# A layer tower of window attention, experts and retention: scores ahead of projection in one loop, retention output ahead of gates in another

## The chip, the cores and the metric

The kernel runs on one core of a Trainium2 chip. The metric is the device time of one execution in microseconds; several executions are timed and their median is compared.

## What is computed

The input is x, 4 x 64 x 64 x 64, that is 16384 tokens of 64 channels. Five parts follow one another; all but the first add to their input.

```python
h = _L0_tok_ref(x, ...)                       # 8x8 windows, rotary attention, 8 heads of 8
h = h + _L0_attn_ref(_layernorm(h), ...)      # 7x7 local attention on the 64x64 grid, 8 heads
h = h + _L0_ffn_ref(_layernorm(h), ...)       # relu(h Wi), two layers of shared + routed expert, Wo
h = h + _L1_attn_ref(_layernorm(h), ...)      # retention: (q k^T / 8 * decay mask) v, causal
h = h + _L1_ffn_ref(_layernorm(h), ...)       # gate > 0.5 over 8 experts, sign(x) @ sign(sum of weights)
```

## The kernel before

All activations stay in one tile `h` (128 partitions, 128 tiles of tokens, 64 channels). Each engine has its own program, written out by hand, and the order of the work on an engine is the order of its code. Engines meet at semaphores that count: `pe.wait_ge(T2["exp_done"], ...)` and the like. An engine that waits holds everything behind it in its program. There are three stages.

The first does the window attention for 32 pieces of 512 tokens. The change does not touch it.

**The merged loop** does the local attention for 64 strips of 4 image rows (256 tokens; index i, in pairs `(j, par)`), and makes, five strips ahead (`LEAD`), the keys, queries and values of strip m = i + 5 from the first stage's rows (the "pre" work). On TensorE (`strip` under `tensor`) a strip is: `scores(0)` (L784, L788), the first half of the attention scores, transposed, into PSUM banks S0 and S1; `peak(.., 0)` (L761, L765), scores of the next strip for its row maxima; `pre_turn` (L733), two transposes of normalized rows; `project` of strip i - 1 (L827); `pre_values` (L741); `scores(1)`, the second half, into the same two banks; `peak(.., 1)`; `values(0)` (L807, L813), sums and weighted values of the first half; `pre_keys` (L749); `turn_maxima` (L773); `values(1)`. ScalarE (`weights`, L1137) takes the exponentials, two instructions for each half, and copies `xnp` (L1093), `v_sb` (L1099), `kpad` (L1104) and `mT` (L1108) out of PSUM; it also issues the loads of `v_patch` (`values_in`, L1126) in its queue. VectorE takes the maxima (L1327), adds the projection to `h` (`residual`, L1341), makes the pre work's statistics (`pre_moments`), and divides the values by their sums (`weigh`, L1332 and L1335, which writes `aT`). GpSimd builds `key_patch` and `q_block` two strips ahead; SP's queue moves keys and queries through memory.

Some waits matter for the change. `project` waits for `attn_out`, that is `aT` of the strip before. `scores(1)` waits until both exponentials of `scores(0)` have read the banks. `values(0)` waits for `v_sb` of the pre values of the same strip, as both use the PSUM bank OT:

```python
if g == 0:
    pe.wait_ge(T2["v_in%d" % par], times((j + 1) * 48))
    pe.wait_ge(T2["attn_out"], times(i))
    pe.wait_ge(L["v_sb"], times(made(j, par)))
```

**The last stage** runs the feed-forward, the retention and the binary experts over 64 strips of 256 tokens as one staggered pipeline: in step j, strip f = j - 1 is in the feed-forward, r = j - 2 in the retention, b = j - 3 gets its retention output added, g = j - 4 its gates, and q = j - 6 its binary weights, 8 units of matmuls (`weights(k)`, L877) into two double banks in turn, each followed by a sign on ScalarE (`sign(k)`, L1165) or, for unit 1, a clip on VectorE (L1416). `reduce` (L894) sums two units. Within a step TensorE does unit 1, transposes (L917), units 2 and 3, the first feed-forward and the gates' matmul (L935, L937), `reduce`, the transposes of the retention's rows (L947) into bank OT, L953, unit 4, the retention's products (L963, L965), unit 5, L985, the spread of x over the gates (L995), L1003, L1005, `w_o` (L1011), unit 6 and `reduce`, unit 7, the retention output (L1027, L1028) into OT, and unit 0 of the next strip. L947 waits until VectorE has added the retention output of step j - 1 to `h` (L1429) from that same bank. VectorE takes the clip, normalizes the retention's rows (L1236), scales them (`kd`, L1421, L1422), compares the gates (L1426, waits for L937), and adds the retention output. SP's queue loads the expert's weights (L451), stores the result (L456) and copies the gated signs `xg` in 12 pieces to where units 0 to 7 read them (L463); the next `xg` (L1452) waits for those copies.

Of the kernel before, what the change touches and what calls it, by code (L numbers as in the profile page):

```python
# [11 lines left out]
ALU = mybir.AluOpType  # L12
# [110 lines left out]
def build(nc, a, out):  # L123
    ctx = ExitStack()
    with ctx:
# [459 lines left out]
        def _(pe):  # L585
# [254 lines left out]
            def strip(j, par):  # L840
                i = j * 2 + par
                m = ahead(j, par)
# [4 lines left out]
                if m is not None:  # L847
                    pre_turn(m)
                if not first:
                    project(i - 1, min(i + LEAD, NS) if isinstance(i, int) else i + LEAD)  # L850
                if m is not None:
                    pre_values(m, 1 - par)
                scores(j, par, 1)
                if not last:
# [13 lines left out]
            def strips(j, par):  # L868
# [128 lines left out]
                if r is not None:  # L997
# [6 lines left out]
                    for t in range(2):  # L1004
                        mm = pe.matmul(bank["OT"][:, 384 + t * C:384 + (t + 1) * C], kd3[:, t, :], v3[:, t, :], start=True, stop=True)  # L1005
                    mm.then_inc(RT["s_ps"], 1)
                if f is not None:
                    pe.wait_ge(FF["hid_sb"], times(f * 3 + 3))
                    settle(pe)
                    for t in range(2):  # L1010
                        mm = pe.matmul(bank["J1"][:, t * C:(t + 1) * C], hidT[:, 2, t * P:(t + 1) * P], w_o[:, :], start=True, stop=True)  # L1011
                    mm.then_inc(FF["out_ps"], 1)

                if q is not None:
                    signed(q, 5)
                    weights(6, par, unit(6, par))
                    reduce(q, 2)
                if g is not None:
# [24 lines left out]
        def _(act):  # L1043
# [84 lines left out]
            def strip(j, par):  # L1128
# [15 lines left out]
                if more:  # L1144
                    values_in(i + 1, 1 - par, 0)
                if m is not None:
                    pre_values(m, j + 2 + par, 1 - par)
                if more:
                    values_in(i + 1, 1 - par, 1)
                weights(1)  # L1150
                if m is not None:
                    pre_keys(m, j + 2 + par, 1 - par)
                if more:
# [5 lines left out]
            def strips(j, par):  # L1159
# [37 lines left out]
                if r is not None:  # L1197
                    act.wait_ge(RT["ud"], times(r + 1))
                    act.activation(v3[:, :, :], bank["OT"][:, 256:384].rearrange("p (t c) -> p t c", t=2), ACT.Copy).then_inc(RT["v"], 1)
                if f is not None:  # L1200
                    act.wait_ge(FF["hid_ps"], times(f * 3 + 3))
                    act.activation(hidT[:, 2, :], bank["J1"][:, 0:256], ACT.Relu, bias=w_exp[:, 1, HID:HID + 1]).then_inc(FF["hid_sb"], 1)

                if q is not None:
                    for k in range(5, 8):
                        sign(k)
# [5 lines left out]
        def _(dve):  # L1212
# [142 lines left out]
            def strip(j, par):  # L1355
# [5 lines left out]
                if not last:  # L1361
                    maxima(i + 1, 0)
                if not first:
                    residual(i - 1)
                if more:
                    pre_moments(nxt)
                if not last:
# [42 lines left out]
            def strips(j, par):  # L1410
# [6 lines left out]
                if r is not None:  # L1417
# [3 lines left out]
                    dve.tensor_scalar(kd3[:, 0, 0:C + 1], xn_r[:, 0, 0:C + 1], decay_k[:, :], None, ALU.mult).then_inc(RT["kd"], 1)  # L1421
                    dve.tensor_scalar(kd3[:, 1, 0:C + 1], xn_r[:, 1, 0:C + 1], decay_k[:, :], keep[:, 0, bass.ds(r, 1)], ALU.mult, ALU.mult).then_inc(RT["kd"], 1)  # L1422
                if g is not None:
                    dve.wait_ge(BN["g_ps"], times(g + 1))
                    dve.wait_ge(BN["xg"], times(g))
                    dve.tensor_scalar(gates[:, :], bank["T"][:, 0:256], b_gate[:, 0:1], 0.0, ALU.add, ALU.is_gt).then_inc(BN["gates"], 1)  # L1426
                if b is not None:
                    dve.wait_ge(RT["out_ps"], times(b + 1))
                    dve.tensor_tensor(rows(b * 2, 2), bank["OT"][:, 256:384].rearrange("p (t c) -> p t c", t=2), rows(b * 2, 2), ALU.add).then_inc(RT["h_done"], 1)  # L1429
                    dve.wait_ge(RT["h_done"], times(b + 1))  # L1430
# [114 lines left out]
```

## Time and profile before

| | |
|---|---|
| median of 3 runs | 1858.53 us (1854.55 to 1858.99) |
| the profiled execution | 1851.32 us, of which the span of instructions is 1849.4 us |
| mean granted clock of TensorE | 0.966 |
| TensorE matmul / weight load busy | 1651.0 us (89%) / 1224.2 us (66%) |
| VectorE, ScalarE, GpSimd busy | 1242.8 us (67%), 978.1 us (53%), 489.4 us (26%) |
| DMA | 139.23 MB, mean 75 GB/s |

Busy time is a share of the whole span and says little about a stage. The first stage ends at about 388 us, the merged loop's strips run from 425 to about 1003 us, the last stage from there to the end, with all its parts at work from about 1060 to 1780 us. The rows below show a wait as "idle before, and who ended it"; "issue" is time for which the profile names nobody. Ends of matmuls are modelled, and each block of matmuls starts some 0.07 to 0.2 us before the modelled end of the one ahead.

### The profile page before, as it was taken

To read this page: it belongs to the slowest core of one execution; us is meant where nothing else is said; L and a number is where in the kernel's file an instruction comes from. 1 tells how busy PE (TensorE), PEld (TensorE's weight loads), DVE (VectorE), ACT (ScalarE), POOL (GpSimd) and SP (SyncE) were. 2 spreads that over 40 slices of the span, in tenths; PEclk is the share of its full clock that TensorE was granted. 3 is DMA by queue.
4 is the path that set the end of the run, shared out by engine and by line. 5 is a ranking of instruction groups with operands and counts; after the bars stand their busy time and mean duration, and the time that the engine had idled before them with its cause. 6 is when DMAs were issued, how large, how long until landed. Compare 5 with 4: busy or idle time off the path is not lost.

```text
span 1849.4 us, 93991 instructions
## 1 busy us (share of the span) xinstructions
PE 1651.0 (89%) x35754; PEld 1224.2 (66%) x35754; DVE 1242.8 (67%) x3477; ACT 978.1 (53%) x1861; POOL 489.4 (26%) x605
## 2 busy tenths in 40 slices
PE   5899999968999999999996799999999999999986
PEld 3566666656777777777775566666666666666663
DVE  2556566655777777777764677777777777777772
ACT  2344444422333333333332277777777777777776
POOL 2200000015555555555542221222122212221210
PEclk8899999968999999999998799999999999999998
DMA  3100000004334444443342133333333333333332
GB/s 97 53 11 14 11 11 11 16 22 112 109 109 112 112 115 113 114 111 110 109 111 61 33 80 80 78 78 83 80 78 77 85 79 78 77 85 78 78 77 60
DMA packets 146983, 139.23 MB, mean 75 GB/s; under 512 B 58754, under 2 KB 106498, under 8 KB 146658
## 3 DMA queue, kind: packets, MB, share of 16 engines
q1 hardware_dynamic: 138594, 112.03, 23.9%
q10 hardware_dynamic: 8320, 26.22, 5.0%
q8 instruction: 50, 0.82, 0.2%
q14 instruction: 19, 0.16, 0.0%
HBM read 62.38 MB, written 16.99 MB: 43 GB/s over the span
## 4 chain that ended last, share of the span: by engine, by line
PE 81%; issue 8%; DVE 5%; SPq 2%; ACT 2%; DMA 1%; POOL 1%; DVEq 0%; ACTq 0%; POOLq 0%
PE ps_D L877 11%; PE ps_D L788 7%; PE ps_OT L807 4%; PE ps_D L666 4%; PE ps_J L827 4%; DVE prob L1416 4%; PE ps_AV L813 3%; PE ps_AV L894 3%; PE ps_D L784 3%; PE ps_J L953 2%; PE ps_J L749 2%; PE ps_OT L741 2%; PE ps_J L985 2%; PE ps_J L620 2%; PE ps_J L935 2%
## 5 line engine op out<-in xcount | busy, mean ns | idle before, releaser
L1165 ACT ACTIVATE prob<-ps_D 128x1024 bf16<-128x1024 f32 x448 | 450.6, 1022 | 80.9 <-PE ps_D L877 80.5
L1137 ACT ACTIVATE prob<-ps_D 100x512 f32<-100x512 f32 x256 | 138.7, 594 | 219.5 <-PE ps_D L788 219.5
L515 POOL TENSOR_TENSOR rstd_pre<-veps_pre,minus_half 128x2 f32<-128x2 f32 x64 | 44.8, 700 | 560.3 <-DVE veps_pre L1224 560.3
L1327 DVE TENSOR_REDUCE m_sb<-ps_D 128x4 f32<-128x400 f32 x256 | 134.6, 567 | 76.4 <-PE ps_D L765 76.3
L788 PE MATMUL ps_D<-tile_a,key_patch 64*100 64x128 f32 x2048 | 174.6, 288 | 1.2 <-issue 1.2
L1290 DVE TENSOR_REDUCE top<-ps_D 128x8 f32<-128x512 f32 x128 | 79.4, 682 | 143.1 <-PE ps_D L639 143.1
L877 PE MATMUL ps_D<-tile_b,w_parts 128*128 128x256 bf16 x1024 | 154.5, 274 | 15.7 <-DVE prob L1416 7.7
L877 PE MATMUL ps_D<-tile_a,w_parts 128*128 128x256 bf16 x1024 | 153.9, 273 | 14.0 <-DVE prob L1416 7.5
L788 PEld LDWEIGHTS ps_D<-tile_a,key_patch 64*100 64x100 f32 x2048 | 136.3, 166 | 1.6 <-issue 1.5
L531 POOL TENSOR_TENSOR tile_a<-q_st,q_mask 128x1024 f32<-128x1024 f32 x64 | 123.5, 1930 | 30.0 <-DMA q_st<-q_d 15.6
L1416 DVE TENSOR_SCALAR prob<-ps_D 128x1024 bf16<-128x1024 f32 x64 | 78.3, 1224 | 76.5 <-PE ps_D L877 76.5
L784 PE MATMUL ps_D<-mT,key_rows 64*100 64x128 bf16 x1024 | 121.3, 227 | 9.2 <-issue 8.7
L515 POOL TENSOR_TENSOR rstd_bin<-veps_bin,minus_half 128x2 f32<-128x2 f32 x64 | 44.1, 689 | 313.4 <-DVE veps_bin L1224 313.4
L877 PEld LDWEIGHTS ps_D<-tile_b,w_parts 128*128 128x128 bf16 x1024 | 87.3, 99 | 55.0 <-issue 42.3
L877 PEld LDWEIGHTS ps_D<-tile_a,w_parts 128*128 128x128 bf16 x1024 | 87.1, 99 | 53.6 <-issue 40.5
L515 POOL TENSOR_TENSOR rstd_ret<-veps_ret,minus_half 128x2 f32<-128x2 f32 x64 | 46.5, 727 | 237.7 <-DVE veps_ret L1224 237.7
L661 PE MATMUL ps_D<-top_T,top_rows 32*64 32x64 bf16 x2048 | 90.3, 193 | 19.6 <-ACT top_T L1071 14.7
L1075 ACT ACTIVATE prob<-ps_D 128x512 f32<-128x512 f32 x128 | 69.5, 595 | 72.1 <-PE ps_D L666 72.0
L894 PE MATMUL ps_AV<-prob,lane_sum 128*32 128x256 bf16 x2048 | 103.4, 279 | 1.2 <-ACT prob L1165 1.2
L1452 DVE TENSOR_TENSOR xg<-ps_D,gates 128x1024 bf16<-128x1024 f32 x64 | 78.3, 1224 | 37.0 <-PE ps_D L995 25.7
L827 PE MATMUL ps_J<-w_p,aT 64*32 64x64 f32 x4096 | 70.4, 217 | 36.5 <-issue 36.5
L827 PEld LDWEIGHTS ps_J<-w_p,aT 64*32 64x32 f32 x4096 | 61.8, 107 | 51.0 <-issue 50.8
(175 smaller groups left out, 3989.7 us busy)
## 6 DMA issues: line engine op xcount, KB each, us to landing
tile_a<-xg SPq DMA_DIRECT2D x384, 64.0 KB, 2.0
tile_b<-xg SPq DMA_DIRECT2D x384, 64.0 KB, 2.0
key_st<-k_d SPq DMA_DIRECT2D x128, 162.0 KB
tile_b<-v_d ACTq DMA_DIRECT2D x128, 120.0 KB
tile_b<-v_d ACTq DMA_DIRECT2D x64, 160.0 KB
w_exp<-experts SPq DMA_DIRECT2D x64, 129.0 KB, 2.3
xin<-in_x SPq DMA_DIRECT2D x32, 128.0 KB, 2.2
k_d<-kpad SPq DMA_DIRECT2D x64, 64.0 KB, 2.8
```

Of the source, the lines that this page charges most:

```text
L515: gp.tensor_tensor(rstd[:, :], veps[:, :], minus_half[:, 0:veps.shape[1]], ALU.pow).then_inc(q["rstd"], 1)
L531: gp.tensor_tensor(q_block[:, par, :].rearrange("c (p h q) -> c p h q", h=NH, q=NQ), q_st[:, :].rearrange("c (p a q) -> c p a q", a=1, q=N ...
L661: pe.matmul(s_tok[j][m, at], top_half(top_rows[r, p * 2 + e, :]), top1_T[r, m], start=True, stop=False)
L784: pe.matmul(s_loc[x][0:NKL, u * P:(u + 1) * P], top_half(key_rows[rows_of(x), par, at * NKL:(at + 1) * NKL]), mT[rows_of(x), par, :], star ...
L788: mm = pe.matmul(s_loc[x][0:NKL, u * P:(u + 1) * P], key_patch[rows_of(x), par, at * NKL:(at + 1) * NKL], q_block[rows_of(x), par, at * P: ...
L827: mm = pe.matmul(bank["J1"][at:at + 32, t * C:(t + 1) * C], aT1[rows_of(x), a4 * P + 32 * r:a4 * P + 32 * (r + 1)], w_p2[rows_of(x), a4, : ...
L877: mm = pe.matmul(d[:, a * 512 + oh * 256:a * 512 + (oh + 1) * 256], w_parts[:, at, oh, :, :].rearrange("r i o -> r (i o)"), x_parts[half][ ...
L894: mm = pe.matmul(bank["AV"][32 * cg:32 * (cg + 1), 0:256], lane_sum[:, int(k == 1), :], sgn[:, k % 4, cg * 256:(cg + 1) * 256], start=k == ...
L1137: act.activation(prob1[0:NKL, 2 * g + x, :], s_loc[x][0:NKL, :], ACT.Exp).then_inc(T2["exp_done"], 1)
L1165: act.activation(sgn[:, k % 4, :], unit(k, par)[:, :], ACT.Sign).then_inc(BN["sign"], 1)
L1327: dve.tensor_reduce(m_sb[:, C * x + HOT[x] + 4 * g:C * x + HOT[x] + 4 * g + 4], m_loc[x][:, 0:4 * NKL].rearrange("p (u n) -> p u n", u=4), ...
L1416: dve.tensor_scalar(sgn[:, 1, :], unit(1, par)[:, :], -TINY, TINY, ALU.max, ALU.min).then_inc(BN["clip"], 1)
```

## The change

In the merged loop, TensorE's `scores(1)` moves from behind `pre_values` to behind `pre_turn`. ScalarE's copy of the pre values moves from between two DMA issues to behind the second exponentials. VectorE's `pre_moments` moves ahead of `residual`.

In the last stage, TensorE's unit 6 and its reduction move ahead of `w_o`, ScalarE's `sign(5)` ahead of the last hidden Relu, and VectorE's add of the retention output ahead of the gates. No instruction is added or taken away.

```diff
@@ merged loop, TensorE
                 if m is not None:
                     pre_turn(m)
+                scores(j, par, 1)
                 if not first:
                     project(i - 1, min(i + LEAD, NS) if isinstance(i, int) else i + LEAD)
                 if m is not None:
                     pre_values(m, 1 - par)
-                scores(j, par, 1)
                 if not last:
                     peak(*after(j, par), 1)
                 values(j, par, 0)
@@ last stage, TensorE
+                if q is not None:
+                    signed(q, 5)
+                    weights(6, par, unit(6, par))
+                    reduce(q, 2)
+
                 if f is not None:
                     pe.wait_ge(FF["hid_sb"], times(f * 3 + 3))
                     settle(pe)
                     for t in range(2):
                         mm = pe.matmul(bank["J1"][:, t * C:(t + 1) * C], hidT[:, 2, t * P:(t + 1) * P], w_o[:, :], start=True, stop=True)
                     mm.then_inc(FF["out_ps"], 1)
-
-                if q is not None:
-                    signed(q, 5)
-                    weights(6, par, unit(6, par))
-                    reduce(q, 2)
@@ merged loop, ScalarE
                 if more:
                     values_in(i + 1, 1 - par, 0)
-                if m is not None:
-                    pre_values(m, j + 2 + par, 1 - par)
-                if more:
                     values_in(i + 1, 1 - par, 1)
                 weights(1)
                 if m is not None:
+                    pre_values(m, j + 2 + par, 1 - par)
                     pre_keys(m, j + 2 + par, 1 - par)
@@ last stage, ScalarE
+                if q is not None:
+                    sign(5)
                 if f is not None:
                     act.wait_ge(FF["hid_ps"], times(f * 3 + 3))
                     act.activation(hidT[:, 2, :], bank["J1"][:, 0:256], ACT.Relu, bias=w_exp[:, 1, HID:HID + 1]).then_inc(FF["hid_sb"], 1)
 
                 if q is not None:
-                    for k in range(5, 8):
+                    for k in range(6, 8):
                         sign(k)
@@ merged loop, VectorE
+                if more:
+                    pre_moments(nxt)
                 if not first:
                     residual(i - 1)
-                if more:
-                    pre_moments(nxt)
@@ last stage, VectorE
+                if b is not None:
+                    dve.wait_ge(RT["out_ps"], times(b + 1))
+                    dve.tensor_tensor(rows(b * 2, 2), bank["OT"][:, 256:384].rearrange("p (t c) -> p t c", t=2), rows(b * 2, 2), ALU.add).then_inc(RT["h_done"], 1)
                 if g is not None:
                     dve.wait_ge(BN["g_ps"], times(g + 1))
                     dve.wait_ge(BN["xg"], times(g))
                     dve.tensor_scalar(gates[:, :], bank["T"][:, 0:256], b_gate[:, 0:1], 0.0, ALU.add, ALU.is_gt).then_inc(BN["gates"], 1)
                 if b is not None:
-                    dve.wait_ge(RT["out_ps"], times(b + 1))
-                    dve.tensor_tensor(rows(b * 2, 2), bank["OT"][:, 256:384].rearrange("p (t c) -> p t c", t=2), rows(b * 2, 2), ALU.add).then_inc(RT["h_done"], 1)
                     dve.wait_ge(RT["h_done"], times(b + 1))
```

How the instructions stand on TensorE in the body of the merged loop before the change, from the pre turn to the first matmuls of `scores(1)` (names of semaphores: `loc_` local attention, `pre_` the pre work; `prob` holds exponentials):

```order
L733 MATMUL ps_T<-ident,xn 64x128 [waits pre_xn,pre_xT_sb]
L733 MATMUL ps_T<-ident,xn 64x128
L827 MATMUL ps_J<-w_p,aT 32x64 [waits loc_h_done,loc_attn_out,pre_k_sb,pre_q_sb]
L827 MATMUL ps_J<-w_p,aT 32x64 x31
L737 REGISTER_ALU
L741 MATMUL ps_OT<-w_v,xnp 128x64 [waits pre_xT_sb,pre_v_sb]
L741 MATMUL ps_OT<-w_v,xnp 128x64
L784 MATMUL ps_D<-mT,key_rows 100x128 [waits loc_exp_done]
L784 MATMUL ps_D<-mT,key_rows 100x128
L788 MATMUL ps_D<-tile_a,key_patch 100x128 x2
```

And in the changed kernel, the same place, from the last matmuls of `scores(1)` to `values(0)`:

```order
L784 MATMUL ps_D<-mT,key_rows 100x128 x2
L788 MATMUL ps_D<-tile_a,key_patch 100x128 x2
L827 MATMUL ps_J<-w_p,aT 32x64 [waits loc_h_done,loc_attn_out,pre_k_sb,pre_q_sb]
L827 MATMUL ps_J<-w_p,aT 32x64 x31
L737 REGISTER_ALU
L741 MATMUL ps_OT<-w_v,xnp 128x64 [waits pre_xT_sb,pre_v_sb]
L741 MATMUL ps_OT<-w_v,xnp 128x64
L757 REGISTER_ALU
L761 MATMUL ps_D<-key_rows,q_rows 128x400 [waits loc_max_done]
L761 MATMUL ps_D<-key_rows,q_rows 128x400
L765 MATMUL ps_D<-key_patch,tile_a 128x100 x8
L807 MATMUL ps_OT<-prob,ones_h 32x4x4x4 [waits loc_exp_done,pre_v_sb,loc_v_in1,loc_attn_out]
```

The scores, whose first matmul waits for `loc_exp_done`, now stand directly behind the pre turn, and between the pre values and `values(0)`, which waits for `pre_v_sb`, only L761 and L765 are left.

VectorE in the last stage before the change, from the clip to the statistics:

```order
L1416 TENSOR_SCALAR prob<-ps_D 128x1024 [waits bin_y_part,bin_w_ps]
L1236 TENSOR_SCALAR xn_r<-h,mv_ret,rstd_ret 128x64 [waits ret_xT_ps,ret_rstd]
L1236 TENSOR_SCALAR xn_r<-h,mv_ret,rstd_ret 128x64
L1421 TENSOR_SCALAR kd<-xn_r,decay_k 128x65 [waits ret_xn,ret_s_ps]
L1422 TENSOR_SCALAR kd<-xn_r,decay_k,keep 128x65
L1426 TENSOR_SCALAR gates<-ps_T,b_gate 128x256 [waits bin_xg,bin_g_ps]
L1429 TENSOR_TENSOR h<-ps_OT,h 128x128 [waits ret_out_ps]
L1218 BN_STATS stats_bin<-h 128x6 [waits ret_h_done]
```

In the changed kernel (where L1425 is the add and L1429 the gates):

```order
L1421 TENSOR_SCALAR kd<-xn_r,decay_k 128x65 [waits ret_xn,ret_s_ps]
L1422 TENSOR_SCALAR kd<-xn_r,decay_k,keep 128x65
L1425 TENSOR_TENSOR h<-ps_OT,h 128x128 [waits ret_out_ps]
L1429 TENSOR_SCALAR gates<-ps_T,b_gate 128x256 [waits bin_xg,bin_g_ps]
L1218 BN_STATS stats_bin<-h 128x6 [waits ret_h_done]
```

The add, which waits for the output of the step before, has changed places with the gates, which wait for this step's matmul.

## Rows read from the trace of the kernel before

**Rows 1.** The page, busy us (share of the span) xinstructions.

```profile
PE 1651.0 (89%) x35754; PEld 1224.2 (66%) x35754; DVE 1242.8 (67%) x3477; ACT 978.1 (53%) x1861; POOL 489.4 (26%) x605
```

**Rows 2.** Stretches: length, busy us (x instructions) by engine, clock, DMA share, GB/s.

```profile
415.00:1000.00 585.00, 529.73 (x16966) 450.47 (x16966) 405.02 (x911) 203.06 (x497) 293.65 (x309) 0.98 0.39 110
1060.00:1780.00 720.00, 667.89 (x6281) 467.54 (x6280) 541.95 (x1981) 547.38 (x869) 148.72 (x234) 1.00 0.33 80
```

**Rows 3.** TensorE's waits, 425 to 1000 us: total us, times, longest.

```profile
PE ps_J L827 <- issue: 34.6, 60, 0.8
```

**Rows 4.** Time line of two strips of the merged loop: start us, us, engine, line.

```profile
707.71 0.26 PE L784 MATMUL ps_D<-mT,key_rows 64*100 64x128 bf16 x2
...
709.19 1.08 ACT L1137 ACTIVATE prob<-ps_D 100x512 f32<-100x512 f32 x2 [1.98 <-PE ps_D L788]
...
709.43 0.41 PE L733 MATMUL ps_T<-ident,xn 128*64 128x128 f32 x2
...
709.71 0.69 DVE L1335 TENSOR_TENSOR aT<-ps_AV,rec 128x512 f32<-128x512 f32 x1
...
710.62 1.10 PE L827 MATMUL ps_J<-w_p,aT 64*32 64x64 f32 x64 [0.78 <-issue]
...
711.64 0.69 PE L741 MATMUL ps_OT<-w_v,xnp 128*128 128x64 f32 x4
...
712.26 0.26 PE L784 MATMUL ps_D<-mT,key_rows 64*100 64x128 bf16 x2
...
712.46 0.28 ACT L1099 ACTIVATE v_sb<-ps_OT 128x128 f32<-128x128 f32 x1 [1.93 <-PE ps_OT L741]
...
713.53 0.34 PE L761 MATMUL ps_D<-key_rows,q_rows 64*128 64x400 bf16 x2
...
713.98 0.65 PE L807 MATMUL ps_OT<-prob,ones_h 100*32 100x64 f32 x32
...
717.12 0.26 PE L784 MATMUL ps_D<-mT,key_rows 64*100 64x128 bf16 x2 [0.27 <-issue]
...
718.68 1.08 ACT L1137 ACTIVATE prob<-ps_D 100x512 f32<-100x512 f32 x2 [2.40 <-PE ps_D L788]
...
722.95 0.65 PE L807 MATMUL ps_OT<-prob,ones_h 100*32 100x64 f32 x32
...
725.75 0.26 PE L784 MATMUL ps_D<-mT,key_rows 64*100 64x128 bf16 x2
```

**Rows 5.** Time line of the last strip: TensorE waits for the exponentials.

```profile
1001.54 1.08 ACT L1137 ACTIVATE prob<-ps_D 100x512 f32<-100x512 f32 x2 [1.96 <-PE ps_D L788]
1002.77 0.44 PE L807 MATMUL ps_OT<-prob,ones_h 100*32 100x64 f32 x17 [0.25 <-ACT prob L1137]
```

**Rows 6.** TensorE's waits, 1060 to 1780 us.

```profile
PE ps_OT L947 <- issue: 32.9, 58, 0.6
```

**Rows 7.** Time line of one step of the last stage.

```profile
1401.12 0.48 DVE L1426 TENSOR_SCALAR gates<-ps_T,b_gate 128x256 f32<-128x256 f32 x1 [0.42 <-PE ps_T L937]
1401.53 0.28 DVE L1429 TENSOR_TENSOR h<-ps_OT,h 128x128 f32 x1
...
1401.91 0.41 PE L947 MATMUL ps_OT<-ident,xn_r 128*128 128x128 f32 x2 [0.53 <-issue]
...
1406.26 1.22 DVE L1452 TENSOR_TENSOR xg<-ps_D,gates 128x1024 bf16<-128x1024 f32 x1 [0.49 <-PE ps_D L995]
...
1407.97 1.94 ACT L1165 ACTIVATE prob<-ps_D 128x1024 bf16<-128x1024 f32 x2 [0.86 <-PE ps_D L877]
...
1409.40 1.25 PE L877 MATMUL ps_D<-tile_a,w_parts 128*128 128x256 bf16 x8
...
1412.16 0.60 PE L877 MATMUL ps_D<-tile_a,w_parts 128*128 128x256 bf16 x4 [0.27 <-DVE prob L1416]
```

**Rows 8.** SP's queue in the same step, in the same time line.

```profile
1408.76 6.26 SPq L463 DMA_DIRECT2D tile_b<-xg  x10
```

**Rows 9.** DMA issues of the page: engine, count, KB each, us to landing.

```profile
tile_b<-xg SPq DMA_DIRECT2D x384, 64.0 KB, 2.0
```

## The prediction, made before the changed kernel was run

> **What bounds the kernel now.** I read the page first: TensorE is busy 1651.0 us of the span, or 89% [rows 1]; no other engine passes 67%. The table of stretches then splits the span: the merged loop, 415 to 1000 us, has TensorE busy 529.73 of 585 us, and the full strips of the last stage, 1060 to 1780 us, 667.89 of 720 us, with a granted clock of 0.98 and 1.00 [rows 2]. So in both stages that the change touches, a microsecond in which TensorE does not stand still is a microsecond of the kernel, and work of the other engines counts only where TensorE waits for it. The list of waits names two such places. In the merged loop TensorE stood idle before `project` (L827) 60 times, 34.6 us in all, 0.58 us each [rows 3]. In the last stage it stood idle before the transposes of L947 58 times, 32.9 us, 0.57 us each [rows 6]. The change aims at both.
>
> The time lines show what ends these waits. In a strip that starts at 707.71 us, TensorE runs first scores, first maxima scores, and the pre turn at 709.43, and is through at about 709.8. `project` needs `aT`, which VectorE writes from 709.71 for 0.69 us, to 710.40; it starts at 710.62 [rows 4]. In the last stage VectorE has waited 0.42 us for the gates' matmul, since 1400.70; gates run 1401.12 to 1401.60, the retention add 1401.53 to 1401.81, and only then, at 1401.91, the transposes start, because they write the PSUM bank that the add reads [rows 7]. The add's own input was made in the strip before. It stands in the queue behind the gates for nothing.
>
> **Part 1, the merged loop.** `scores(1)` is put into the gap, ahead of `project` and `pre_values`. Nothing is added: blocks of TensorE change places, so only waits can change. Lengths, start to start [rows 4]: project 711.64 - 710.62 = 1.02; pre values 712.26 - 711.64 = 0.62; scores 713.53 - 712.26 = 1.27; maxima scores 713.98 - 713.53 = 0.45. Together 3.36 from project to `values(0)`.
>
> The new order has two waits. First, `scores(1)` writes the two banks that the exponentials of `scores(0)` read. They run 709.19 to 710.27, and from the end of an exponential to TensorE it is 0.15 us (1002.62 to 1002.77 [rows 5]), so `scores(1)` starts at 710.42, where `project` started at 710.62: 0.20 us earlier. In the next strip, which starts after the loop's branch, they end at 719.76, so it starts at 719.91; `project` started 3.36 before 722.95, at 719.59: 0.32 us later. Project itself then waits for nothing: it comes 1.27 us after that, and `aT` was there at 710.40.
>
> Second, `values(0)` waits for the copy `v_sb` of the pre values, since they share a PSUM bank. Today that copy ends 712.74, 1.10 us after the pre values started, hidden by scores(1). Behind the pre values there now stand only the maxima scores: 0.62 + 0.45 = 1.07 us, against 1.10 + 0.15 = 1.25. That is a new wait of 0.18 us in each strip. ScalarE's new order (the copy behind the second exponentials) costs nothing: exponentials end 2.56 us after their scores start (707.71 to 710.27 [rows 4]), and the pre values are done 1.27 + 1.02 + 0.69 = 2.98 us after `scores(1)` starts.
>
> So one strip of a pair changes by -0.20 + 0.18 = -0.02 and the other by +0.32 + 0.18 = +0.50; a pair, today 9.41 + 8.63 = 18.04 us, grows by 0.5. Over 29 pairs that is +14 us. In the last five strips there is no pre work. There `project` now lies beside the exponentials and hides their wait; moved behind, its 1.02 us come on top: +5, less 1 for the first strip, where the pre values today wait for their copy. The merged loop: **+18 us**. The queues: on ScalarE the second DMA issue of `v_patch` moves ahead of the copy, some 1.5 us earlier, at a time when the queue waits anyway. VectorE's `pre_moments` before `residual` costs nothing: after the first maxima VectorE would stand until `project`, which ends 1.3 us later than now, and the moments (about 1 us) fill that. It hides `residual` from `maxima(1)` as before, and GpSimd gets its input sooner.
>
> A rule of the Trainium skill (Perfetto Trace Analysis, Matmuls) speaks against this part: independent groups of matmuls should rotate through PSUM banks, so that the evacuation of one lies under the next group. Here two groups that use the same two banks come together. By that rule taken alone all of the 1.08 us of exponentials would be bare, and this is the last rival below.
>
> **Part 2, the last stage.** The add ahead of the gates: it runs from 1400.70 for 0.28 us, to about 1401.0, and nothing in it waits. The gates still start at 1401.12, when their matmul is done. So the transposes follow the block before them (0.53 us recorded as gap, 0.60 counted start to start, since blocks overlap by 0.07 [rows 7]): TensorE comes **0.59 us** earlier. What is late next? I walked one strip with the durations of today. (a) Unit 6 of the gate weights and its reduction move ahead of `w_o`, and on ScalarE `sign(5)` ahead of the last hidden Relu. Today sign 6 and 7 run 1407.97 to 1409.91, and the second half of the eight weight matmuls from 1409.40 (unit 1 of the next strip) needs sign 7: ScalarE is level with TensorE there [rows 7]. With the move unit 6 is about 0.46 us, one block of `w_o`, sooner, sign 6 starts about 1.05 us earlier and sign 7, behind unit 7, some 0.6; unit 1 then starts on time or 0.02 late. Without the move sign 7 would stand behind sign 6 and come 0.05 later: the move is worth little. (b) Unit 7 waits for `xg`, 1406.26 to 1407.48; that shifts by 0.6 with TensorE, and unit 7 too. (c) Unit 3 waits for the clip on VectorE, 0.27 us as now [rows 7]: it hangs on unit 1 and shifts with it. (d) The next `xg` waits for twelve copies of this one by SP's queue. They start at 1408.76, ten issues take 6.26 us, and one lands 2.0 us after its issue [rows 8, 9]: the last at 1408.76 + 11 x 0.626 + 2.0 = 1417.6. The next `xg` starts at 1406.26 + 12.4 = 1418.7 (58 steps in 720 us are 12.4 each [rows 2, 6]). In the new order that is 1.2 us sooner (twice 0.6), and the copies only 0.4, as SP first takes the expert's weights behind the last hidden Relu. Of 1.0 us in hand 0.2 is left. (e) `w_o` comes 0.86 us later against its neighbours; `h` of the feed-forward is added after the state update anyway, and its statistics have over a microsecond before the next use.
>
> Thus 58 strips by 0.59 = 34 us, and 1 for the strips at both ends: **-35 us**.
>
> **Sum.** +18 - 35 = -17 us. The profiled execution took 1851.3 us; it would take 1834. The median of the runs is 1858.5, 7 us above the profiled one; against it the forecast is **1841.5 us**, 0.9% faster. A difference of 0.3% (5.6 us) is what a measurement of this kernel can tell.
>
> **Rivals.**
> 1. *The last stage gives only half.* Speaks for it: three things are level within 0.1 us after the walk (sign 7, the state update before L1027, the copies by SP's queue). If any is 0.3 us later than I think, the gain is 0.3 a strip, 17 us. Then +18 - 17: about 1859 us. Against: each was taken with measured durations. Chance 0.15.
> 2. *The merged loop costs nothing.* If the wake of TensorE overlaps its weight load, or the exponentials start sooner, both new waits shrink by 0.15 and the gain of the even strip cancels the loss. Then -35: about 1824 us. Chance 0.16.
> 3. *The exponentials lie bare* (the slower one). Place: before `scores(1)` in the merged loop. The first maxima scores (0.45) and the pre turn (0.41, less 0.07 of overlap) are 0.79 us of work under the exponentials. If they are held themselves (by the maxima or by GpSimd's patches), the cover is gone and each of 63 strips pays 0.79 more, 50 us: 1858.5 - 17 + 50 = 1891 us. It decides from 0.36 us of lost cover a strip, where 23 us more bring the sum to +0.3%. Against: in rows 4 the turn follows without a gap, and nothing that feeds it moves later. Chance 0.07.
>
> **Numbers.** Forecast 0.62, rivals 0.15, 0.16, 0.07. The forecast's own spread is 1830 to 1853 (merged loop +8 to +25, last stage -36 to -30). The range 1824 to 1860 takes in rivals 1 and 2 and leaves out rival 3 and the far tails. Faster by over 0.3%: nearly all of the forecast, rival 2 and a little of rival 1, 0.79; within 0.3%: most of rival 1 and the edge of the forecast, 0.12; slower: rival 3 and the rest of 1, 0.09.
>
> **What would show it.** The idle time before L947 gone from the waits, gates behind the add, and a full step of the last stage 0.6 us shorter than today's 12.4. In the merged loop: no idle before `project`, but about 0.6 us before the second scores and 0.1 to 0.2 before `values(0)`, and a pair of strips of 18.5 us instead of 18.04. The forecast is wrong if a pair takes 18.1 or less (rival 2), if those steps stay above 12.05 us (rival 1), or if the gap before the second scores passes 1.1 us (rival 3).

## The result

The kernel before takes 1858.16 us (median; 1854.55 to 1858.99), the changed one 1843.87 us (1842.19 to 1845.71). The ratio is 0.9927, 95% interval 0.991 to 0.9944: 0.7% faster, where 0.9% was forecast. The profiled execution of the changed kernel took 1842.19 us, its span is 1840.2 us, 9.1 less than before.

The page, busy us by engine, answers to [rows 1]:

```profile
PE 1665.6 (91%) x35754; PEld 1227.2 (67%) x35754; DVE 1202.4 (65%) x3477; ACT 976.0 (53%) x1861; POOL 488.3 (27%) x605
```

The table of stretches, with the columns of [rows 2]:

```profile
415.00:1000.00 585.00, 524.53 (x16217) 436.10 (x16219) 359.45 (x910) 198.85 (x492) 288.26 (x309) 0.98 0.41 108
...
1060.00:1780.00 720.00, 696.14 (x6467) 490.01 (x6467) 569.54 (x2093) 560.58 (x902) 158.74 (x246) 0.99 0.34 82
```

TensorE's busy time in 720 us of the last stage rose from 667.89 to 696.14; in 585 us of the merged loop it fell from 529.73 to 524.53 (the changed kernel enters this loop 6.5 us later in its profile, see below). One stage gained and the other lost.

TensorE's waits from 425 to 1030 us, the merged loop (total us, times, longest), against [rows 3]:

```profile
PE ps_D L784 <- ACT prob L1137: 41.0, 64, 1.3
PE ps_D L784 <- issue: 8.7, 28, 1.5
```

The 34.6 us before `project` (L827) are gone. In their place stand 41.0 us before the second scores (L784), which wait for the exponentials. The `issue` row of L784 is the loop's branch, 0.27 us in every other strip, as in [rows 4].

Two strips on the time line, as in [rows 4]:

```profile
714.25 0.26 PE L784 MATMUL ps_D<-mT,key_rows 64*100 64x128 bf16 x2 [0.26 <-issue]
...
715.81 1.08 ACT L1137 ACTIVATE prob<-ps_D 100x512 f32<-100x512 f32 x2 [2.39 <-PE ps_D L788]
...
717.04 0.26 PE L784 MATMUL ps_D<-mT,key_rows 64*100 64x128 bf16 x2 [0.66 <-ACT prob L1137]
...
718.40 1.10 PE L827 MATMUL ps_J<-w_p,aT 64*32 64x64 f32 x64
...
719.43 0.68 PE L741 MATMUL ps_OT<-w_v,xnp 128*128 128x64 f32 x4
...
720.04 0.35 PE L761 MATMUL ps_D<-key_rows,q_rows 64*128 64x400 bf16 x2
720.15 0.28 ACT L1099 ACTIVATE v_sb<-ps_OT 128x128 f32<-128x128 f32 x1 [0.48 <-PE ps_OT L741]
...
720.64 0.65 PE L807 MATMUL ps_OT<-prob,ones_h 100*32 100x64 f32 x32
...
721.67 0.70 PE L749 MATMUL ps_J<-xnp,w_kq 128*128 128x256 f32 x2
...
722.20 0.27 PE L773 MATMUL ps_T<-ident,m_sb 128*128 128x128 f32 x1
722.41 0.65 PE L807 MATMUL ps_OT<-prob,ones_h 100*32 100x64 f32 x32
...
723.44 0.26 PE L784 MATMUL ps_D<-mT,key_rows 64*100 64x128 bf16 x2
...
726.15 0.26 PE L784 MATMUL ps_D<-mT,key_rows 64*100 64x128 bf16 x2 [0.58 <-ACT prob L1137]
```

The exponentials end at 716.89, the second scores start at 717.04: the forecast 0.15 us. `values(0)` starts 0.21 us after the `v_sb` copy ends (720.43 to 720.64); 1.21 us after the pre values.

TensorE's waits from 1070 to 1750 us, the last stage, against [rows 6]:

```profile
PE ps_D L877 <- DVE prob L1416: 4.0, 26, 0.2
...
PE ps_OT L947 <- DVE h L1425: 0.6, 1, 0.6
```

The wait before L947 is gone but for one. A step of the last stage, against [rows 7, 8]:

```profile
1400.76 0.48 DVE L1429 TENSOR_SCALAR gates<-ps_T,b_gate 128x256 f32<-128x256 f32 x1 [0.29 <-PE ps_T L937]
...
1400.95 0.44 PE L947 MATMUL ps_OT<-ident,xn_r 128*128 128x128 f32 x2
...
1407.84 1.02 ACT L1163 ACTIVATE prob<-ps_D 128x1024 bf16<-128x1024 f32 x1 [0.26 <-PE ps_D L877]
1408.00 7.54 SPq L463 DMA_DIRECT2D tile_a<-xg  x12
...
1408.47 1.13 PE L877 MATMUL ps_D<-tile_b,w_parts 128*128 128x256 bf16 x8
...
1409.19 1.02 ACT L1163 ACTIVATE prob<-ps_D 128x1024 bf16<-128x1024 f32 x1 [0.33 <-PE ps_D L877]
...
1410.36 1.34 PE L877 MATMUL ps_D<-tile_b,w_parts 128*128 128x256 bf16 x8
...
1411.90 0.28 DVE L1425 TENSOR_TENSOR h<-ps_OT,h 128x128 f32 x1
...
1412.41 0.48 DVE L1429 TENSOR_SCALAR gates<-ps_T,b_gate 128x256 f32<-128x256 f32 x1 [0.22 <-PE ps_T L937]
...
1412.60 0.44 PE L947 MATMUL ps_OT<-ident,xn_r 128*128 128x128 f32 x2
```

The transposes start without a wait, one step after the other by 1412.60 - 1400.95 = 11.65 us. The add (L1425) stands ahead of the gates.

Where the 9.1 us of the two spans come from, by TensorE's first instructions: the first stage, whose code is the same, is 6.5 longer (431.75 against 425.25 us up to the first scores; in the twelve profiles of this study it ends anywhere from 423.3 to 433.5); the merged loop, up to the last stage's first transposes (L917), takes 611.2 instead of 588.0 us, **+23.2**; from there to the last L917 764.2 instead of 803.9, **-39.7**; the end +0.9. Without the first stage the two profiles differ by 15.6 us, close to the 14.3 us between the medians.

### The profile page after: what moved, and what is told of

Same layout as the page of the kernel before. It is cut to its first block, busy times and chain, and to the rows that moved or that the text cites. A ratio compares the mean times of both kernels' runs of the same rounds, so it can differ in the third digit from the quotient of the medians.

```text
span 1840.2 us, 93991 instructions
## 1 busy us (share of the span) xinstructions
PE 1665.6 (91%) x35754; PEld 1227.2 (67%) x35754; DVE 1202.4 (65%) x3477; ACT 976.0 (53%) x1861; POOL 488.3 (27%) x605
## 4 chain that ended last, share of the span: by engine, by line
PE 78%; issue 7%; DVE 5%; ACT 4%; SPq 3%; POOL 1%; DMA 1%; DVEq 0%; ACTq 0%; POOLq 0%
PE ps_D L877 10%; PE ps_D L788 7%; PE ps_OT L807 4%; PE ps_D L666 4%; PE ps_J L827 4%; DVE prob L1416 3%; PE ps_AV L813 3%; SPq L463 3%; PE ps_AV L894 3%; PE ps_D L784 3%; ACT prob L1137 2%; PE ps_J L749 2%; PE ps_OT L741 2%; PE ps_J L620 2%; PE ps_AV L676 2%
## 5 line engine op out<-in xcount | busy, mean ns | idle before, releaser
L1163 ACT ACTIVATE prob<-ps_D 128x1024 bf16<-128x1024 f32 x448 | 459.5, 1029 | 123.0 <-PE ps_D L877 121.4
L784 PE MATMUL ps_D<-mT,key_rows 64*100 64x128 bf16 x1024 | 126.6, 224 | 50.1 <-ACT prob L1137 41.0
L877 PE MATMUL ps_D<-tile_b,w_parts 128*128 128x256 bf16 x1024 | 150.9, 272 | 15.1 <-DVE xg L1453 5.5
L877 PE MATMUL ps_D<-tile_a,w_parts 128*128 128x256 bf16 x1024 | 152.7, 275 | 10.8 <-DVE prob L1416 3.9
L788 PEld LDWEIGHTS ps_D<-tile_a,key_patch 64*100 64x100 f32 x2048 | 143.0, 165 | 1.0 <-issue 1.0
L784 PEld LDWEIGHTS ps_D<-mT,key_rows 64*100 64x100 bf16 x1024 | 75.8, 123 | 72.0 <-issue 68.6
L877 PEld LDWEIGHTS ps_D<-tile_b,w_parts 128*128 128x128 bf16 x1024 | 91.8, 102 | 47.8 <-issue 37.4
L877 PEld LDWEIGHTS ps_D<-tile_a,w_parts 128*128 128x128 bf16 x1024 | 92.8, 103 | 43.6 <-issue 32.5
L661 PEld LDWEIGHTS ps_D<-top_T,top_rows 32*64 32x64 bf16 x2048 | 75.8, 108 | 28.9 <-issue 28.9
```

The costliest lines, as they stand in the source:

```text
L661: pe.matmul(s_tok[j][m, at], top_half(top_rows[r, p * 2 + e, :]), top1_T[r, m], start=True, stop=False)
L784: pe.matmul(s_loc[x][0:NKL, u * P:(u + 1) * P], top_half(key_rows[rows_of(x), par, at * NKL:(at + 1) * NKL]), mT[rows_of(x), par, :], star ...
L788: mm = pe.matmul(s_loc[x][0:NKL, u * P:(u + 1) * P], key_patch[rows_of(x), par, at * NKL:(at + 1) * NKL], q_block[rows_of(x), par, at * P: ...
L877: mm = pe.matmul(d[:, a * 512 + oh * 256:a * 512 + (oh + 1) * 256], w_parts[:, at, oh, :, :].rearrange("r i o -> r (i o)"), x_parts[half][ ...
L1163: act.activation(sgn[:, k % 4, :], unit(k, par)[:, :], ACT.Sign).then_inc(BN["sign"], 1)
```

## The experiments

Where one says a pair, it is the mean over the 27 pairs of strips 3 to 57, from one first scores to the next: 18.09 us before, 18.73 with the change. A step is the mean of 54 steps of the last stage: 12.35 and 11.67 us. All were timed beside the kernel before on their chip.

### e1 and e2: each part alone

e1 is the whole change without the edit below and its matching moves on ScalarE and VectorE. e2 is the kernel before with this edit and these moves alone:

```diff
                     pre_turn(m)
+                scores(j, par, 1)
                 if not first:
                     project(i - 1, min(i + LEAD, NS) if isinstance(i, int) else i + LEAD)
                 if m is not None:
                     pre_values(m, 1 - par)
-                scores(j, par, 1)
```

> The merged loop is as before the change, only the last stage is changed. Theory A (the last stage gains, the merged loop loses): 58 steps of 11.65 us instead of 12.35, so about 39 us less than before, 1819 us, and some 24 us less than the changed kernel; pairs of strips in the merged loop back at 18.09 us. Theory B (the merged loop is level, and the whole 14 us came from the last stage): about 1844 us, as the changed kernel.

> Only the merged loop is changed. Theory A: pairs of strips at 18.72 us instead of 18.09, over 29 pairs 18 us, and 4 to 6 us in the last strips: about 1881 us, slower than before by 1.2%. Theory B: within 3 us of before, 1858 us. The last stage keeps its 12.35 us a step and 0.57 us of idle time before the transposes.

Measured: e1 1819.57 us (1818.58 to 1822.81), ratio to before 0.9811 (0.9786 to 0.9835); e2 1880.10 us (1877.57 to 1884.27), ratio 1.0136 (1.0108 to 1.0164). Pairs take 18.14 in e1 and 18.72 in e2, steps 11.67 and 12.35. TensorE's largest waits from 425 to 1030 us, of e1 and of e2:

```profile
PE ps_J L827 <- issue: 37.3, 60, 2.0
```

```profile
PE ps_D L784 <- ACT prob L1137: 39.4, 61, 1.3
```

Theory A holds in both. The parts add up: -1.9% and +1.4%, and the whole is -0.7%. The merged loop's new order is a loss by itself, and half the change beats the whole.

### e3 and e4: the two edits of the last stage

e3 keeps of the change only the add ahead of the gates on VectorE, e4 only unit 6 ahead of `w_o` with `sign(5)` ahead of the Relu:

```diff
+                if b is not None:
+                    dve.wait_ge(RT["out_ps"], times(b + 1))
+                    dve.tensor_tensor(rows(b * 2, 2), ...)
                 if g is not None:
                     dve.wait_ge(BN["g_ps"], times(g + 1))
```

> Only the add of the retention output stands ahead of the gates. Theory A (the wait before the transposes is the whole gain, unit 6 is worth at most 0.05 us a step): a step of 11.7 to 11.8 us, 1822 to 1826 us. Theory C (sign 6 would hold sign 7 and unit 1, so that unit 6 ahead of w_o is worth 0.1 us or more a step): a step of 11.85 us or longer, 1829 us or more.

> Only unit 6, its reduction and sign 5 are moved. Theory A: nothing, 12.35 us a step, 1858 us. Theory C: unit 1 of the next strip starts 0.1 us sooner, since sign 7 no longer stands behind sign 6, so a step of 12.25 us and about 1852 us. The 0.57 us before the transposes stay in both.

Measured: e3 1826.05 us, ratio 0.9846 (0.982 to 0.9872); e4 1850.99 us, ratio 0.9974 (0.9953 to 0.9995). Steps, from the profiles: 11.75 in e3 (0.60 less than before), 12.27 in e4 (0.08 less). TensorE's waits from 1070 to 1750 us, of e3 and of e4:

```profile
PE ps_D L877 <- DVE prob L1416: 14.0, 53, 0.3
```

```profile
PE ps_OT L947 <- issue: 31.8, 56, 0.6
PE ps_D L877 <- DVE prob L1418: 3.8, 25, 0.2
```

For e3 theory A came true, for e4 theory C. The add gives nearly nine tenths of the gain. Unit 6 is worth 0.08 us a step. The eight matmuls of units 0 and 1 take 1.13 us (1408.47) and not 1.25 [rows 7], since `sign(7)` (1407.84 to 1408.86 in the changed kernel) is done before the second half, unit 1, needs it. The clip before unit 3 is waited for 4 us in all and not 14, but that is no second gain: it hangs on unit 1, and unit 2 ahead of it now starts later. Unit 2 needs `sign(0)` (1409.19 to 1410.21) and starts 0.15 us behind it, at 1410.36. In means over some 50 steps of e3 and of the changed kernel, units 0 and 1 take 1.17 and 1.05 us, from the transposes (L917) to unit 2 it is 0.39 and 0.50, and from unit 2 to L935 1.38 and 1.27. So 0.12 us is gained in all, and the block of `w_o`, 0.46 and now 0.52 us long, takes a part of it back.

### e5: is the wait for `v_sb` a loss?

The changed kernel with one move on TensorE:

```diff
-                values(j, par, 0)
                 if m is not None:
                     pre_keys(m, 1 - par, i)
+                values(j, par, 0)
```

> The changed kernel with one move on TensorE in the merged loop: the block of pre keys goes ahead of values(0), so that it runs while ScalarE copies v_sb. Theory A (the merged loop lost a wait of about 0.2 us per strip for v_sb ahead of values(0), and TensorE sets the pace of a strip): the wait is filled, 0.2 to 0.25 us less per strip, merged pairs near 18.3 instead of 18.72, 12 to 15 us over the loop: 1829 to 1832 against 1843.9. Theory B (the wait ahead of values(0) only takes up time that the next wait would have cost): pairs stay at 18.7 and the time within 3 us of 1843.9; the wait before scores(0) or before scores(1) grows by what is gained here.

Measured: 1840.56 us (1837.54 to 1843.48), ratio 0.9898 (0.9866 to 0.993), which overlaps the changed kernel's interval; a pair 18.70. TensorE's blocks on the time line of e5:

```profile
718.39 0.35 PE L761 MATMUL ps_D<-key_rows,q_rows 64*128 64x400 bf16 x2
...
718.85 0.70 PE L749 MATMUL ps_J<-xnp,w_kq 128*128 128x256 f32 x2
...
719.48 0.65 PE L807 MATMUL ps_OT<-prob,ones_h 100*32 100x64 f32 x32
...
720.51 0.33 PE L773 MATMUL ps_T<-ident,m_sb 128*128 128x128 f32 x1
...
720.77 0.65 PE L807 MATMUL ps_OT<-prob,ones_h 100*32 100x64 f32 x32
```

The wait is filled: keys follow the maxima scores after 0.46 us, where `values(0)` followed them after 0.60. But keys, first values, turn of the maxima now take 0.63 + 1.03 + 0.26 = 1.92 us to the second values, and values, keys, turn took 1.03 + 0.53 + 0.21 = 1.77. From maxima scores to second values it is 2.38 against 2.37. Theory B forecast the pair rightly, but its reason was wrong: no other wait took over. In over 50 strips of e5 the keys take 0.63 us and the turn 0.26, the same to 0.01 each time, as they would not if waits stood in them. So **what was gained in the wait was lost at the seams between the blocks**: the same block is longer or shorter according to the block behind it.

### e6: what the wait before the second scores costs

In the changed kernel the exponentials of the first half take 256 of their 512 columns; the other weights are left out.

```diff
+                        n = 256 if g == 0 else 512
-                        act.activation(prob1[0:NKL, 2 * g + x, :], s_loc[x][0:NKL, :], ACT.Exp)...
+                        act.activation(prob1[0:NKL, 2 * g + x, 0:n], s_loc[x][0:NKL, 0:n], ACT.Exp)...
```

> The changed kernel, whose exponentials of the first half of each strip of the merged loop take 256 of the 512 columns (the other half of those weights is left out). It prices the wait before the second scores. Theory A (the second scores start 0.15 us after the second exponential of the first half ends, and nothing else ends that wait): each of the two exponentials is about 0.25 us shorter, the wait of 0.6 to 0.7 us per strip is gone, the scores behind it last 1.27 again and not 1.36, pairs fall by 1.1 to 1.4 us, the time by 35 to 45 us to 1799 to 1809. Theory B (the wait is taken over by the next one, v_sb ahead of values(0) or the next maxima, because ScalarE and VectorE have their own chain round the strip): less than half of it is gained, 1825 or more.

Measured: 1816.39 us (1814.71 to 1819.58), ratio 0.9779 (0.9747 to 0.9811); a pair 17.89, 0.84 less. ScalarE and TensorE's waits (425 to 1030 us) in e6:

```profile
706.94 0.66 ACT L1138 ACTIVATE prob<-ps_D 100x256 f32<-100x256 f32 x2 [1.98 <-PE ps_D L788]
...
709.58 1.08 ACT L1138 ACTIVATE prob<-ps_D 100x512 f32<-100x512 f32 x2 [1.50 <-DMA v_d<-v_sb]
```

```profile
PE ps_D L784 <- ACT prob L1138: 12.6, 55, 0.9
```

The two exponentials take 0.66 us together and not 1.08, and a strip becomes 0.42 us shorter, all of it. So the wait is the exponentials' and its price was real. The size was forecast too large, 1.1 to 1.4 us a pair and 35 to 45 in all, where 0.84 and 27 came. I had counted 0.25 us less for each exponential, and each gave 0.21; 0.2 us of wait a strip remains; and the second scores, which were to last 1.27 us again without the wait, still last 1.36. It also shows what comes next: the second exponentials do not follow the scores, but a DMA of the stores, for ScalarE's queue holds the value loads ahead of them.

### e7 and e9: an order without the two waits

e7 is e1's last stage with the merged loop in another order: projection between first maxima and turn, keys ahead of `values(0)`, and on VectorE the attention's weighing ahead of the pre norm, so that `aT` is there in time. ScalarE keeps the order of the change, and VectorE adds the projection ahead of the moments, as before the change.

```diff
                     peak(*after(j, par), 0)
+                if not first:
+                    project(i - 1, ...)
                 if m is not None:
                     pre_turn(m)
                 scores(j, par, 1)
-                if not first:
-                    project(i - 1, ...)
```

```diff
                 if m is not None:
                     pre_queries(m, j + 2 + par, 1 - par)
+                weigh(i)
                 if more:
                     pre_norm(nxt)
-                weigh(i)
```

> The last stage as in the change, the merged loop in a third order: TensorE runs the projection and the pre turn between the first maxima block and the second scores, pre values behind the second scores, pre keys ahead of values(0); ScalarE's order as in the change, VectorE weighs ahead of the pre norm. Theory A (the time of a merged strip is TensorE's blocks plus its waits; with about 2 us of other blocks between the two scores and keys under the v_sb copy no wait is left): a pair takes about 17.3 instead of the 18.09 of the order before, 25 us less than the kernel with only the last stage changed (1819.6): near 1794. Theory B (another chain round the strip, VectorE's or ScalarE's, sets the pace at 18 us a pair): within 5 us of 1819.6, with waits for the turn or the maxima in place of those removed.

Measured: 1835.70 us (1830.56 to 1837.85), ratio 0.9868 (0.9834 to 0.9902); a pair 18.76: 16 us slower than e1. Neither theory had this. A strip of e7 on the time line:

```profile
716.90 0.26 PE L784 MATMUL ps_D<-mT,key_rows 64*100 64x128 bf16 x2
...
717.59 1.38 ACTq L1126 DMA_DIRECT2D tile_b<-v_d  x2
...
718.26 0.69 PE L741 MATMUL ps_OT<-w_v,xnp 128*128 128x64 f32 x4
...
719.16 1.08 ACT L1137 ACTIVATE prob<-ps_D 100x512 f32<-100x512 f32 x2 [1.70 <-DMA v_d<-v_sb]
...
720.13 0.28 ACT L1099 ACTIVATE v_sb<-ps_OT 128x128 f32<-128x128 f32 x1
...
720.62 0.65 PE L807 MATMUL ps_OT<-prob,ones_h 100*32 100x64 f32 x32 [0.58 <-issue]
```

The second scores wait for nothing any more (716.90 follows the turn). But the second exponentials start at 719.16, 0.9 us after TensorE has gone on to the pre values (718.26): ScalarE first waits for the stores that the two value loads need, and then issues the loads, 1.38 us. The `v_sb` copy is queued behind them and ends at 720.41, and `values(0)` starts 0.21 us later. The waiting place was again one that I had not walked, a DMA issue on a compute engine's queue. The Trainium skill (Perfetto Trace Analysis, What "DMA-bound" means) names the issuing engine's sequencer as one place where DMA can bind, and says that the window recorded there is descriptor generation and not data movement. The ACTq row is such a window; what it costs the compute instructions queued behind it is shown by e9.

e9 puts the loads behind:

```diff
+                weights(1)
+                if m is not None:
+                    pre_values(m, j + 2 + par, 1 - par)
                 if not isinstance(i, int) or i + 2 < NS:
                     act.wait_ge(L["stored%d" % par], times((j + 2) * 48))
                 if more:
                     values_in(i + 1, 1 - par, 0)
                     values_in(i + 1, 1 - par, 1)
-                weights(1)
                 if m is not None:
-                    pre_values(m, j + 2 + par, 1 - par)
                     pre_keys(m, j + 2 + par, 1 - par)
```

> The kernel of e7 with one more move on ScalarE: the second exponentials and the v_sb copy go ahead of the two value loads (and of the wait for the stores that these loads need). In e7's profile the second scores end at 4.83 us of a strip, but the second exponentials start only 0.65 us later, behind the loads' issues, and values(0) waits 0.48 to 0.66 us for the v_sb copy that is queued behind them. Theory A (that queue is what ate e7's gain): the exponentials start 0.1 us after the scores, values(0) follows the keys without a wait, pairs fall from 18.76 to 17.6 to 17.8, the time by 28 to 33 us to 1803 to 1808, below the 1819.6 with only the last stage changed. Theory B (ScalarE's copy of the maxima for the next scores(0), now queued behind the loads, becomes the wait): scores(0) waits longer, pairs 18.2 or more, 1820 or more.

Measured: **1800.68 us** (1795.5 to 1806.87), ratio to before 0.9709 (0.9674 to 0.9744); a pair 17.61. TensorE's waits from 425 to 1030 us:

```profile
PE ps_J L827 <- issue: 9.9, 32, 2.0
PE ps_D L784 <- issue: 8.4, 28, 1.3
```

Theory A came true: the pair is at the lower end of what it gave, the time 2 us below it, by a move in one queue that changes no arithmetic. From the keys to `values(0)` it is now 0.63 us in the mean and was 1.20 in e7, which is the whole difference of 1.15 us a pair. What is left is the branch and, in every other strip, 0.24 us before `project`, which starts 0.22 us after `aT` is written (717.69 to 717.91 on e9's time line). This beats both kernels and e1.

### e8: VectorE's order by itself

The changed kernel with VectorE's order as before:

```diff
                 if not last:
                     maxima(i + 1, 0)
+                if not first:
+                    residual(i - 1)
                 if more:
                     pre_moments(nxt)
-                if not first:
-                    residual(i - 1)
```

> The changed kernel with VectorE's order in the merged loop as it was before (residual ahead of the pre moments), TensorE's and ScalarE's changed. Theory A (VectorE waits for the projection, which now comes later, and the pre moments, the second maxima and the pre norm are queued behind it): TensorE's next turn or second scores wait longer, 0.1 to 0.6 us per strip, 1850 to 1880. Theory B (VectorE has slack enough): within 3 us of 1843.9; the change of VectorE's order does nothing by itself.

Measured: 1854.58 us (1848.42 to 1865.14), ratio 0.9991 (0.9966 to 1.0017); a pair 19.21, 0.24 us more a strip. TensorE's waits in the loop:

```profile
PE ps_D L761 <- POOL key_patch L540: 34.2, 55, 0.8
```

The moments behind the residual make GpSimd's inverse deviation late (GpSimd waits 5.02 us for it on e8's time line, 3.41 in the changed kernel's), and behind that in its queue stand the query block and the key patches of the next first maxima scores (L761). The time came out as theory A gave it, the place did not: the stretch from first scores to first maxima scores grows from 1.25 to 2.05 us in the mean, while that from the turn to the second scores shrinks from 1.03 to 0.39. With TensorE's order of the change, the move on VectorE is a needed part; e9, where the projection comes earlier on TensorE, does without it.

### e10: the price of a seam

The kernel of e5 with one block moved on:

```diff
                 scores(j, par, 1)
+                if not last:
+                    peak(*after(j, par), 1)
                 if not first:
                     project(i - 1, ...)
                 if m is not None:
                     pre_values(m, 1 - par)
-                if not last:
-                    peak(*after(j, par), 1)
                 if m is not None:
                     pre_keys(m, 1 - par, i)
```

> The kernel of e5 with TensorE's second maxima block moved to right behind the second scores, ahead of the projection. It prices a seam: in every trace so far the scores block lasts 1.24 to 1.27 us up to a maxima block behind it, and 1.36 up to a projection or pre values, with and without a wait ahead of it. Theory A (the seam, not the wait ahead, makes the block longer): 1.27 again from second scores to second maxima, 0.09 us less per strip, pairs 18.5 against 18.70, 5 us less time: about 1835. Theory B (the length comes with the wait ahead of the block): 1.36 stays, and pairs are within 0.05 of 18.70.

Measured: 1848.94 us (1843.59 to 1855.44), ratio 0.9965 (0.9951 to 0.998); a pair 18.96. The time line and the wait list of e10:

```profile
712.17 0.26 PE L784 MATMUL ps_D<-mT,key_rows 64*100 64x128 bf16 x2 [0.66 <-ACT prob L1137]
...
713.41 0.37 PE L761 MATMUL ps_D<-key_rows,q_rows 64*128 64x400 bf16 x2
...
715.82 0.67 PE L749 MATMUL ps_J<-xnp,w_kq 128*128 128x256 f32 x2 [0.21 <-DVE h L1341]
```

Theory A is right on the seam: the second scores last 713.41 - 712.17 = 1.24 us with a wait of 0.66 ahead, and e7 has 1.36 (716.90 to 718.26) with none ahead. As a forecast of the time it failed, with 1848.94 for 1835: a new wait of 0.2 us stands before the keys, which need the residual, and the stretch from pre values to keys, 0.28 us longer than the pre values were in e5, takes more than the 0.12 that the seam gave.

## Why the prediction held, point by point

- **Merged loop, +18: right in its places, 5 us short.** The second scores start 2.79 us after the first (714.25 to 717.04), and 2.71 in the other strip (723.44 to 726.15); forecast were 2.79 and 2.71, from rows of before alone. The wait for `v_sb` came too (1.21 us from pre values to `values(0)` in the strip shown, 1.25 in the mean; forecast 1.25). A pair grew by 0.64 us and not 0.5. Means of over 50 strips say where a strip grew, from start to start: the turn with the wait behind it from 0.99 to 1.03 us, the second scores from 1.27 to 1.36, the second maxima scores with the wait for `v_sb` from 0.45 to 0.64, everything else by 0.01 or less. The step that was mis-sized is the length of the scores block, taken over as 1.27 us; with the projection behind it, it lasts 1.36 (717.04 to 718.40), 0.09 a strip, some 5 us over the loop. The last strips cost 6 and not 5 (+3.9 from strip 57 to 63, +2.0 behind), and the 1 us taken off for the first strip was not there: strip 3 starts 29.3 us after strip 0 in both kernels.
- **ScalarE's and VectorE's moves at no cost: right.** The copy of the pre values comes in time, as its row (720.15) has ScalarE waiting 0.48 us for the matmuls. e8 adds that VectorE's is needed.
- **The add ahead of the gates, 0.59 us a step: right**, 0.60 in e3.
- **(a) Unit 6 "worth little", 0.05 at most: mis-sized.** It is 0.08 us a step, 5 us. The walk saw that sign 7 and unit 1 are level and counted only the 0.05 by which sign 7 would slip further; it missed that unit 1 already stood 0.12 us in every step for `sign(7)`, and that the move takes this away. (c) held for the add alone, where the wait for the clip stays (14.0 us in e3); with unit 6 moved it is 4.0. A step is thus 0.68 us shorter (12.35 to 11.67), where 0.59 was forecast, and the stage gives 40 us and not 35.
- **(d) SP's queue, 0.2 us in hand: none is.** The `xg` copies start at 1408.00 and twelve issues take 7.54 us, to 1415.54; the next `xg` starts at 1417.00, and VectorE's row names the copies as what it waited for. The row and VectorE's waits from 1070 to 1750 us:

```profile
1417.00 1.22 DVE L1453 TENSOR_TENSOR xg<-ps_D,gates 128x1024 bf16<-128x1024 f32 x1 [0.49 <-DMA tile_a<-xg]
```

```profile
DVE xg L1453 <- DMA tile_a<-xg: 15.4, 29, 1.6
...
DVE xg L1453 <- DMA tile_b<-xg: 12.3, 26, 0.7
```

TensorE hardly waits behind it (L877 for `xg` twice, 0.9 us in all): unit 7 starts at 1418.85, 0.63 us after `xg` ends. So this miss cost nothing here. The queue is probably the next bound of the last stage, which is argued and not shown; a kernel with this queue relieved was not tried.
- **Rival 1** (half the gain) fell: steps 11.67, against its bound of 12.05. **Rival 2** (the merged loop free) fell: 18.73 a pair, against 18.1. **Rival 3** (exponentials bare) fell: 0.66 us of wait and not 1.08; turn and first maxima stayed under them. The rule on rotating banks in the Trainium skill (Perfetto Trace Analysis, Matmuls) was right in direction all the same. Both waits of the new order stand between two users of the same bank, but the one for the exponentials only takes the place of the one before `project` (0.04 us a strip more); what lost this part is the wait for `v_sb` in bank OT (0.19) and the longer scores block (0.09).

The two size errors, +5 and -5, cancel, and that is luck. The forecast 1841.5 lies 2.4 us from 1843.87, in part by that.

## What to carry to other kernels

Price the parts of a change apart: here one part gave 37 us and the other took back 23 of it, and only e1 and e2 show that from the outside. When a block is moved into a gap, ask which wait it meets there; the gap before `project` was 0.58 us and the one before the second scores 0.64 (41.0 us, 64 times). Before the order of one engine is changed, walk the queues of the others with the new times, their DMA issues too: e7 and e9 have the same order on TensorE and differ by 35 us.

## What the runs showed of the hardware

**Seams.** The same 24 matmuls of a scores block last 1.24 to 1.27 us up to a maxima block and 1.36 up to a projection or pre values, whatever is ahead of them. Why is not shown. The order of blocks on TensorE alone moved 0.15 us a strip (e5).

**VectorE beside GpSimd.** The pre norm's instructions (L1236) lie under GpSimd's copies before, and behind them with the change. Of before and of after, min/median/max ns:

```profile
L1236 DVE TENSOR_SCALAR xn<-h,mv_pre,rstd_pre x116: 300/752/1181, 436.3 to 952.7; 128x64 f32 x112, 128x64 f32<-128x64 f32 x4
```

```profile
L1236 DVE TENSOR_SCALAR xn<-h,mv_pre,rstd_pre x116: 306/314/1071, 440.9 to 975.8; 128x64 f32 x112, 128x64 f32<-128x64 f32 x4
```

The same instruction takes 0.31 us alone and 0.75 under `key_patch` copies: before, each of the 116 lies beside such a copy; with the change, 111 lie beside no GpSimd instruction, and these take 0.32 us at most. That agrees with the Trainium skill (SBUF — State Buffer, Who interferes with whom), by which VectorE and GpSimd share one pair of ports under an exclusive lock. Here it cost nothing that the wait lists show, since TensorE waited for `xn` in neither kernel.
